# Row maxima carried by DMA, one block of each sum through the matrix unit, the second norm on ScalarE, in a kernel of two cross-attention layers

## The reference

```
def layer0(x, context):                      # x (4,1024,512), context (4,1024,384)
    h = (x - mean) * rsqrt(var + 1e-5) * gamma + beta
    Q, K, V = h @ Wq, context @ Wk, context @ Wv        # 16 heads of 64
    attn = softmax(Q K^T) * 64 ** -0.5                  # scaled after the softmax
    return x + (attn V) @ Wo + bo

def layer1(x, enc):                          # enc is the same context
    xn = x * rsqrt(mean(x * x) + 1e-5) * norm_w
    q = xn @ wq;  k, v = split(enc @ wkv)               # 16 heads of 32
    q, k = l2_normalize(rotate(q)), l2_normalize(rotate(k))
    attn = softmax(q k^T * sqrt(32))
    return x + (attn v) @ wout
```

## Time and profile before

| | |
|---|---|
| device time, median of 3 runs | 3294.47 us (3291.69 to 3295.61) |
| the profiled execution | 3299.25 us, of which the span is 3297.5 us |
| PE busy | 3101.0 us, 94% of the span |
| DVE busy | 2336.7 us, 71% |
| ACT busy | 1396.3 us, 42% |
| POOL busy | 485.3 us, 15% |
| DMA, hardware queue | 102.6 MB, 11.7% of 16 engines |
| PE clock granted, mean | 0.984 of full |

### The profile page before, as it was taken

How to read it: one execution, slowest core, us unless ns; L and a number is a source line. 1 busy time by engine, 2 the same in 40 slices (tenths; PEclk the granted TensorE clock), 3 DMA queues, 4 the chain that set the end, 5 groups by cost and what they waited for, 6 DMA issues and landing times.

```text
span 3297.5 us, 73037 instructions
## 1 busy us (share of the span) xinstructions
PE 3101.0 (94%) x31708; PEld 1575.8 (48%) x31708; DVE 2336.7 (71%) x2580; ACT 1396.3 (42%) x1472; POOL 485.3 (15%) x221
## 2 busy tenths in 40 slices
PE   6999999899899999989989999999999999999997
PEld 3555555454355455544345555554434455555441
DVE  3677776687776776678777777767877777776876
ACT  1333333456433333355633333335563333334564
POOL 1000002352000000335100000024410000012430
PEclk8999999999999999999999999999999999999999
DMA  3001000201111010011111110101111101000001
GB/s 110 15 25 26 21 25 16 59 21 40 45 51 28 21 25 21 22 51 27 40 45 47 28 25 21 25 15 57 24 40 59 36 21 25 25 24 19 21 16 37
DMA packets 178405, 107.28 MB, mean 33 GB/s; under 512 B 81452, under 2 KB 147116, under 8 KB 178088
## 3 DMA queue, kind: packets, MB, share of 16 engines
q1 hardware_dynamic: 178088, 102.60, 11.7%
HBM read 93.12 MB, written 9.42 MB: 31 GB/s over the span
## 4 chain that ended last, share of the span: by engine, by line
PE 84%; DVE 8%; issue 3%; ACT 2%; DMA 2%; SPq 1%; POOL 0%; DVEq 0%; ACTq 0%; POOLq 0%
PE scores L682 20%; PE o_acc L694 19%; PE work L721 12%; PE work L715 11%; PE work L759 10%; PE work L650 5%; DVE acc L853 3%; PE work L752 2%; PE work L742 2%; DVE tile_max L837 1%; ACT probs L786 1%; PE work L747 1%; PE work L769 1%; DVE stats L873 1%; DMA rows_dram<-sums 0%
## 5 line engine op out<-in xcount | busy, mean ns | idle before, releaser
L786 ACT ACTIVATE probs<-scores 128x1024 f32<-128x1024 f32 (+1 forms) x768 | 980.9, 1309 | 533.3 <-PE scores L682 524.3
L853 DVE TENSOR_TENSOR acc<-acc,probs 128x1024 f32<-128x1024 f32 (+1 forms) x576 | 932.4, 1619 | 22.6 <-DVE acc L853 0.9
L837 DVE TENSOR_REDUCE tile_max<-work 128x2 f32<-128x1024 f32 x496 | 607.1, 1224 | 476.2 <-PE work L650 473.1
L694 PE MATMUL o_acc<-probs,v_tok 128*64 128x512 f32 (+1 forms) x4096 | 777.1, 610 | 0.2 <-ACT probs L786 0.2
L968 POOL TENSOR_TENSOR inv<-sumsq,power 128x16 f32<-128x16 f32 x64 | 186.5, 2914 | 2040.8 <-DVE sumsq L916 2040.4
L759 PE MATMUL work<-wo,o_sum 128*32 128x512 f32 (+1 forms) x2072 | 404.8, 610 | 60.1 <-issue 40.4
L682 PE MATMUL scores<-q_high,k_high 32*128 32x512 f16 (+1 forms) x2048 | 310.2, 395 | 25.9 <-ACT probs L786 12.9
L938 DVE TENSOR_TENSOR resid<-work,resid 128x512 f32<-128x512 f32 x384 | 262.1, 686 | 101.2 <-PE work L759 101.0
L694 PEld LDWEIGHTS o_acc<-probs,v_tok 128*64 128x64 f32 (+1 forms) x4096 | 165.4, 122 | 347.0 <-issue 335.3
L682 PE MATMUL scores<-q_high,k_low 32*128 32x512 f16 (+1 forms) x2048 | 303.0, 385 | 0.0
L682 PE MATMUL scores<-q_low,k_high 32*128 32x512 f16 (+1 forms) x2048 | 302.0, 383 | 0.0
(11 more groups left out here) (76 smaller groups left out, 2709.8 us busy)
## 6 DMA issues: line engine op xcount, KB each, us to landing
recip<-rows_dram SPq DMA_DIRECT2D x380, 64.0 KB, 2.2
stage<-in_x_dram SPq DMA_DIRECT2D x8, 1024.0 KB, 7.1
wq<-in_L_xattn_Wq_dram SPq DMA_DIRECT2D x32, 256.0 KB, 2.7
resid<-in_x_dram SPq DMA_DIRECT2D x8, 1024.0 KB, 5.2
wo<-in_L_xattn_Wo_dram SPq DMA_DIRECT2D x32, 256.0 KB, 2.7
out_dram<-resid SPq DMA_DIRECT2D x8, 1024.0 KB, 4.3
wk<-in_L_xattn_Wk_dram SPq DMA_DIRECT2D x32, 192.0 KB, 2.5
wv<-in_L_xattn_Wv_dram SPq DMA_DIRECT2D x32, 192.0 KB, 2.5
```

The lines of the kernel that those rows point to most:

```text
L694: mm = pe.matmul(o_acc[h * d:(h + 1) * d, :], v_tok[par][:, kt, h * d:(h + 1) * d], probs[:, unit_slot(t, n, kt, h // 2), h % 2, :], start ...
L786: act.activation(block_probs(t, n, kt), scores[:, 2 * (no % 2):2 * (no % 2) + g, :], ACT.Exp, scale=(1.0, float(D1) ** 0.5 / QK_SCALE ** 2 ...
L837: dve.tensor_reduce(tile_max[:, qt, :, n:n + 1], maxima_banks(e), AX.X, ALU.max, negate=True).then_inc(dve_freed, 1)
L853: dve.tensor_tensor(a, block_probs(t, n, 0) if kt == 1 else a, block_probs(t, n, kt), ALU.add).then_inc(add_ok, units)
```

## The change

1. **Maxima by DMA.** For turns 0 to 6, except the first half of turn 0, the entry `T` becomes `rows`. DVE reduces the maxima into `neg_rows` (8 numbers on each partition); SP writes them to DRAM element by element (1024 elements of 4 bytes), waits until they have landed, and reads them back as two rows of 512 into partitions 0 and 64 of `shift`. `shift` is set to zero once, at the start. These are 13 halves of each sequence, 52 in all. The 3 others of each sequence keep the products.
2. **Last block of layer 1.** DVE no longer adds block 7 of a half of layer 1 to `acc`. PE adds it by four more products with ones, straight from `probs`, in the bank of `den` (32 halves). `den` of a half before a half of layer 1 moves to the end of the step before; `recip` and `norm_o` of those halves move to the end of steps 1 and 3.
3. **Second norm on ScalarE.** The four row scalings of `norm_b` of layer 1 become four ACT instructions, and DVE has none of them.
4. **Tables anew.** Around the change of layer (turns 6 and 7) `kT`, `kr` and `den` are moved; the load of the next sequence goes from step 1 to step 2 of its half; `ct` and `xt` of the next sequence are spread one by one over the steps; the `R` of the next sequence begin two steps earlier and stand one or two to a step, where there were two to a step.

```diff
-            (6, 1): [E("T", t7, 1), [], [], E("kT", t8, 0, 1) + E("norm_a", (b, 1), 0) + E("kr", t9, 0)],
-            (7, 1): [E("norm_b", (b, 1), 0) + lead("v", t8, 0) + transposed(1, b, 0, 0, 1, 2, 3) + E("v", t8, 0) + E("qr", t8, 0),
-                     E("v", t8, 1) + E("kr", t9, 1), E("qT", t8, 0), []]}[p, n]
+            (6, 1): [E("T", t7, 1), [], E("kT", t8, 0, 1), E("norm_a", (b, 1), 0)],
+            (7, 1): [E("kr", t9, 0) + transposed(1, b, 0, 0, 1, 2, 3) + lead("v", t8, 0) + E("qr", t8, 0),
+                     E("v", t8, 0) + E("v", t8, 1), E("qT", t8, 0) + E("kr", t9, 1), []]}[p, n]
...
-        more = {(1, 0): ((1, E("load_x", nb, 0, 1) + E("load_c", nb, *range(C_RING))),),
+        more = {(1, 0): ((2, E("load_x", nb, 0, 1) + E("load_c", nb, *range(C_RING))),),
...
-        ends = (0, 0, 0, 0, 0, 0, 0, 2, 4, 6, 8, 10, 12, 14, 16, 16, 16)
+        ends = (0, 0, 0, 0, 0, 1, 2, 4, 5, 6, 8, 9, 11, 12, 14, 16, 16)
...
+        if j > 0 and l == 1:
+            steps[-1].fill += E("den", *HALVES[j - 1])
+        if (l, p, n) == (0, 7, 1):
+            half[0].early += E("norm_b", (b, 1), 0)
...
+            def send_shift(t, half):
+                out_no = rows_sent(t, half)
+                sp.wait_ge(neg_max_ok, 2 * turn0_no(t) + half + 1)
+                with nc.allow_non_contiguous_dma("single maxima"):
+                    sp.dma_start(shift_rows[half].rearrange("(a p) -> p a", p=P), neg_rows[:, :, :].rearrange("p h j -> p (h j)").bitcast(F32)).then_inc(shift_out, 16)
+                sp.wait_ge(shift_out, 16 * out_no)
+                sp.dma_start(shift[t % 2][0:D0 + 1:D0, tokens(half)].bitcast(F32), shift_rows[half].rearrange("(h n) -> h n", h=G0)).then_inc(shift_in[half], 16)
...
+                    if l == 1:
+                        pe.wait_ge(exp_ok, UNIT_NO[e.t, e.i, KT - 1, UNITS_OF[e.t] - 1] + 1)
+                        for h in range(g):
+                            mm = pe.matmul(w[h * d:(h + 1) * d, :], ones[l][:, 0:d], block_probs(e.t, e.i, KT - 1)[:, h, :], start=False, stop=True)
...
+            def row_scale(b, half):
+                act.wait_ge(work_full, ITEM["xt", (b, 0), (XC - 1, half)].full)
+                act.wait_ge(rstd_ok, norm_no((b, 1), half))
+                for t in range(half * HT, half * HT + HT):
+                    a = act.activation(stage[:, t, :], resid[:, t, :], ACT.Copy, scale=rstd[:, t:t + 1])
+                a.then_inc(xn_ok[1], 1)
```

More of the change, by code:

```diff
@@ L150, in layer1_beside, with by_products, shifts_loaded, rows_sent @@
     return s
+def by_products(t, half):
+    return TURN[t][2] == 7 or (TURN[t][2], half) == (0, 0)
+def shifts_loaded(t, half):
+    return sum(not by_products(i, half) for i in range(t + 1) if TURN[i][1] == 0)
+def rows_sent(t, half):
+    return shifts_loaded(t, 0) + shifts_loaded(t - (half == 0), 1)
 def maxima_beside(t, n):
@@ L173, in maxima_beside, with add_results @@
     return [r[ends[i]:ends[i + 1]] for i in range(4)]
-def add_results(half, t, n, beside, maxima):
+def add_results(half, t, n, beside):
     b, l, p = TURN[t]
@@ L180, in add_results @@
     if len(half) == 8:
[L181 to L184, removed]
+        beside[1] += E("recip", t, n)
+        at = len(beside[3]) - (beside[3][-1].kind in ("kr", "qr") if beside[3] else 0)
+        beside[3][at:at] = E("norm_o", t, n)
         each = 2 if (l, p) == (0, TURNS0 - 1) else 1
@@ L240, in make_plan @@
         for i, st in enumerate(half):
+            for e in beside[i]:
+                if e.kind == "T" and not by_products(e.t, e.i):
+                    e.kind = "rows"
             at = 1 if len(maxima[i]) == 1 and not (l == 1 or (p, n) == (7, 1)) else len(maxima[i]) - 1
@@ L362, in norm_no, with norm_of_layer_no @@
     return 4 * b + 2 * l + half + 1
+def norm_of_layer_no(which, half):
+    return 2 * which[0] + half + 1
 def build(nc, rows, x, ctx_in, wq0, wk0, wv0, wo0, bo, gamma, beta, norm_w, wq1, wkv1, wout1,
@@ L465, in build @@
         rstd_ok = sem("rstd_ok")
-        xn_ok = sem("xn_ok")
+        xn_ok = [sem(f"xn_ok{l}") for l in range(2)]
         work_full = sem("work_full")
@@ L471, in build @@
         neg_max_ok = sem("neg_max_ok")
+        shift_out = sem("shift_out")
+        shift_in = [sem(f"shift_in{i}") for i in range(2)]
         scores_ok = sem("scores_ok")
@@ L766, in entry @@
                     c, half = e.i
[L767 removed]
+                    pe.wait_ge(xn_ok[e.t[1]], norm_of_layer_no(e.t, half))
                     for j in range(HT):
@@ L783, in scored @@
                     act.wait_ge(av_ok, block_no(*before[:3]))
-                    act.wait_ge(add_ok, adds_after(*before))
+                    if before[2] > last_sum(before[0]):
+                        act.wait_ge(work_full, (ITEM.get(("den", *before[:2])) or ITEM["den_end", before[0], before[1]]).full)
+                    else:
+                        act.wait_ge(add_ok, adds_after(*before))
                 act.wait_ge(scores_ok, last + 1)
@@ L951, in entry @@
                     row_stats(e.t, e.i)
-                elif e.kind == "norm_b":
+                elif e.kind == "norm_b" and e.t[1] == 0:
                     row_norm(e.t, e.i)
+            for i in range(2):
+                dve.memset(shift[i][:, :].bitcast(F32), 0.0)
             dve.memset(ones[0][:, :], float(D0) ** 0.5)
```

56 lines of the change are left out of this document (36 added, 20 removed).

## The result

The changed kernel takes 3686.28 us (median; 3685.56 to 3688.59), the kernel before 3293.39 beside it: ratio 1.1189, 95% interval 1.1175 to 1.1202. It is 12% slower. The forecast was 3254 with a range of 3220 to 3302.

A forecast was written before the change was run, and what follows sets the result against it. PE was taken as the bound, busy 3101.0 of 3297.5 us. Terms -44.7 + 27 - 14 - 43 + 11 = -64, with 24 lost to the DMA -40, took the median 3294.5 to 3254 us, range 3220 to 3302.

The forecast's parts named there:

- The time of the single elements (L): SP's wait in layer 0 for the maxima's write to land: taken as 3.8 us, ends 2.8 and 6.3; 24 us lost.
- The formula: Layer 0: `norm_o` ready 8.2 + L behind sums, due 11.7; each us of L beyond 3.5 costs PE one in 47 halves.
- SP becomes the bound of layer 0: Rival, chance 0.17: in layer 0 the wait for the single elements holds the reciprocals; at L 6.3, 3362 us.
- point of decision (4.9 us): In layer 0, the L from which SP's wait for the single elements eats the whole gain.
- Products that go: Layer 0: 52 `T` leave PE, 50.4 us, less 5.7 lost as `R` waits for its bank; gain 44.7 us.
- PE busy lower by about 18 us: Sign over the whole kernel that the prediction is right: PE's busy time falls by about 18 us.
- The load a step later: Load of the next sequence: `recip` goes before it, ending three PE waits at the `out` of about 5.2 us; 14 gained.
- Products with ones and the tables: Layer 1's four added products in 32 halves lose 27 us; waits covered, mostly around the change of layer, gain 43.
- the rival of moved waits: Rival, chance 0.13: waits at the change of layer move to another late engine; of 57 us only 15 come, 3296.
- Second norm on ACT: Turns 7 and 8: ACT's scalings delay the scores, 9 us lost, plus 2 from the other half: 11 us lost.
- The wait of 3.9 for the scores: First half of turn 8: PE waits 3.9 us for the exponential behind ACT's four scalings, against 1.3 before.
- Sum without the DMA: Whole kernel: all terms except the 24 us lost to the maxima's DMA, together -64 us.

The follow-up runs named there:

- experiment 3: Changed kernel with the maxima's write behind the reciprocals, written in other forms and spacings: 1024 elements adjacent 8.8 to 9.7 us, 64 bytes apart 2.6; total not compared.
- packed_ahead: Changed kernel with maxima written as 128 runs of 32 bytes ahead of the sums, without SP waiting, read back in two DMAs behind the reciprocals: 3258.05 us, ratio 0.9884.
- load_later: Kernel before with one number changed, the load of the next sequence in step 2 of its half instead of step 1: 3280.28 us, ratio 0.9956.
- packed_ahead_norm_dve: packed_ahead with the second norm's scaling put back on DVE: 3226.43 us, ratio 0.9786 against the kernel before.
- before_packed: Kernel before with only the later load and the maxima of turns 0 to 6 by the DMA of packed_ahead: 3235.46 us, ratio 0.9819.

## Why the prediction was wrong, point by point

- **The time of the single elements (L), the step that failed.** I put it at 3.8 us, between 2.8 and 6.3, by runs of 16 bytes and by reads of single elements. It is 8.9. The first row puts four writes into a 64-byte stretch where the single elements put sixteen, and the second is of reads; by experiment 3 the crowding of the writes makes most of the difference (3.6 us with four to a stretch, about 9 with sixteen). The bounds were drawn from rows whose form differed in the property that decides.
- **What L costs.** The formula held. It puts `norm_o` 8.2 + 8.9 = 17.1 us behind the sums; the rows show 254.86 - 237.30 = 17.56. Its loss of 47 x (8.9 - 3.5) = 254 us compares with 324.8 - 23.0 = 302 us of PE's waits at the `out`, 6.4 in each half against 5.4. Two things were no terms of it. The product of maxima of turn 7 waits for DVE, which stands behind `norm_o` in its order (29.0 us in 4 against 3.0 before: 26 us). And PE runs at the half clock behind such waits: busy 3183.5 against 3082.6 in `packed_ahead`, 101 us for the same instructions. 302 + 26 + 101 = 429; by the spans of these two executions the kernels are 425 apart (324 us of idle time and 101 of busy time).
- **The rivals.** "SP becomes the bound of layer 0" was the right mechanism, with its place. Its point of decision (4.9 us) was not tried in the place of the change; the forms of experiment 3 that landed near it (4.5 and 5.9 us) were only measured beside it. Its price (3362) was too low, for L and for the clock. It got 0.17, because I weighed the 2.2 and 2.8 of the reciprocals above the 4.2 and 6.3 of the single elements. The latter were explained away by loads beside them.
- **The page.** The rule of the Trainium skill's page "DMA: Bandwidth & Descriptors", section "Rules for kernel authors", that a non-contiguous last dimension makes one descriptor per element, spoke against the change, as I had written. The trace agrees with it in the count: the packets under 512 bytes rise from 81452 to 135636, by 1042 for each of the 52 DMAs. But the price is not in the count alone, since the same 1024 elements apart land in 2.6 us. The section "Anatomy of one DMA" of the same page of the Trainium skill gives its 2 us for DMAs that GpSimd issues, while all of these are SP's. It comes near for `recip` (2.1) and not for adjacent single elements (8.9). The same page of the Trainium skill says in its section "Specifications" that below 512 bytes a DMA does a read-modify-write. Steps of that kind, one behind another where writes crowd, would fit the table of experiment 3, which no run shows directly; a size under 512 bytes alone doesn't explain it, since runs of 32 bytes land in 1.9.
- **Products that go.** Forecast 44.7 us, measured 44.8 by the medians and 36 by the profiled spans. The sum is borne out; that it agrees to 0.1 us is luck. (The sign "PE busy lower by about 18 us" counted 5.7 us of waiting as busy time: 50.4 less 27 is 23.)
- **The load a step later.** Forecast 14, measured 14 (0.44% of 3294, interval 9 to 20). In part this is luck. I left 0.5 us of each wait at the `out`; in `load_later` 1.9 is left at the first place, and the waits at the `out` fall by 10.7 us in all (40.4 to 29.7). PE's busy time falls too (3101.0 to 3088.2), since behind the wait of 5.42 us the granted clock had been 0.63 for 6 us, a term that I had not counted.
- **Products with ones and the tables.** Forecast 27 - 43 = -16; `packed_ahead_norm_dve` less `before_packed` is -9 by medians and -4.8 by spans; by their intervals this is uncertain by some 8 us either way, so that the parts tell more than the sum. PE's busy time is up by 22.9 us, near the 27. Its idle time is down by 27.7, not 43. `q_low` (11.5 in `before_packed`) and `c_ring` (9.3, now 0.7) went as forecast, and the `stage` wait with the norm on DVE too (12.8). `tile_max` fell from 38.1 to 31.1, where 13 was forecast, and a new wait came: PE for DVE's last `acc` (9.7 us in 8 where it was 1.0), which the rival of moved waits had in mind.
- **Second norm on ACT.** Forecast 11, measured 27 to 32. The wait of 3.9 for the scores was 3.3, so the row was read rightly. The clock behind it (7 us of busy time) was no term, and the 6.7 us of `stage` in the other half, where I had counted 2, were mis-sized. I had also set 1.3 us against each wait for the norm on DVE, but in `packed_ahead_norm_dve` that wait is gone: the changed tables remove it, so there was nothing to set off.
- **Sum without the DMA.** Forecast -64. Measured -36 (`packed_ahead`). Of the 28 us that are missing, some 16 to 21 are the norm's and 7 to 11 the tables'. So the sign of the case turned on one number, of a write that no row of the trace showed.

## What to carry to other kernels

Where a cost has no row in the trace, don't bound it by rows that are near in size but differ in form, and work out from which value on the sign turns: if a form never measured could lie beyond it, that chance is large. A transpose through DRAM should write each partition's numbers as one run and do its single elements on the reading side, with both sides sent where nothing urgent stands behind them on the queue. Count for a wait of PE of several us also the stretch at half clock behind it.

## What the runs showed of the hardware

- What a DMA of separate small writes to DRAM costs depends most on how closely they crowd. 1024 single elements of 4 bytes take 2.6 us when 64 bytes apart, 3.1 at 32 bytes, 3.6 at 16, 4.5 to 5.9 at 8, and 8.8 to 9.7 when adjacent. 128 adjacent ones take 6.9, more than 1024 that lie 8 bytes or more apart.
- Such a write, adjacent, also delays what its queue sends next: the sums land in 4.9 us in the median half and in up to 10.3, where 1.6 is usual.
- A read of single elements holds the issue of the next DMA: 3.35 us where 0.37 is usual (1024 elements in one DMA), about 1.1 behind two DMAs of 512.
- Behind 6 us without work TensorE's granted clock was 0.56 for 6 us; behind 3.3 us it was 0.68 for 5.4. After these stretches it was 1.00 again in both. Over the changed kernel that is 101 us, a quarter of its loss.
